# A two-layer attention kernel on one core: additions on GpSimd split into two instructions of two heads each, and TensorE's program put into a loop

## Chip, cores, metric

The kernel runs on one core of a Trainium2 chip. The metric is the device time of one execution in microseconds; the median of three runs is given. All numbers are f32.

## What is computed

For each of 32 images of 128 channels and 32 x 32 = 1024 tokens, the reference computes three stages:

```
x = x + conv_attention(group_norm(x))          # L0: one head of 128 channels, 1024 x 1024 weights
t = tokens(x)
t = t + retrieval_attention(layer_norm(t))     # L1: 8 heads of 16 channels, 1024 x 1024 weights each
t = t + (layer_norm(t) @ w_lora.T) @ W.T       # w_lora is decoded from 4-bit codes
```

In L1, `search_attn = softmax(sq @ sk.T)` for each of the 8 heads, `retrieved = search_attn @ rv` for 2 sets of values, and a small second softmax mixes the two sets. The kernel does not normalise the L1 weights: it takes exponentials of the scores, multiplies them with the values, adds them up over the keys for the denominators, and divides behind that.

## The kernel before

**Phases and steps.** The eight heads of an image are two groups of four (`GROUP = 4`), the 1024 queries are two halves. A group and a half are a phase, so an image has four phases. A phase runs over 8 key tiles of 128 keys; one phase and one key tile are a step, 32 steps an image. In a step TensorE computes four score tiles of 128 keys x 512 queries (`scores`, L791, two entries of two heads each), ACT takes their exponentials out of PSUM into a place of the ring `p1[:, step % 4, n, :]` (L965, four instructions), TensorE multiplies every two steps with the values into `ps_u` (`values`, L805), and GpSimd adds the place to the running sum `p_sum` (`add`, L647), one instruction of 128 x 2048 a step. The first addition of a phase adds the places of steps 0 and 1, so there are 7 a phase and 28 an image. At the end of a phase TensorE multiplies the sum with ones (`den`, L814), ACT copies it out (`den_sb`, L976) and TensorE turns it (`turn_den`, L822).

**The maxima.** Before that TensorE computes the same scores with queries in the rows (`max1`, L771, 64 entries of two matmuls an image), and DVE reduces each bank to a maximum (L1085).

**Order.** Each engine has its order for one turn written out as text (`PE_ORDER`, `ACT_ORDER`, `DVE_ORDER`, `POOL_ORDER`, `SP_ORDER`). An entry such as `scores.8@0/34` is stage, index, how many images ahead of the turn, and for TensorE the PSUM banks. A turn holds 222 entries of TensorE and work of three or four images. `in_order` walks the order: the first turns and the last ones, in which entries of images that don't exist are left out, are written out; the turns between are a loop on the device (`nc.Fori`, 28 turns, with a hint for the back edge) on ACT, DVE, GpSimd and SyncE. TensorE's call has `loop=False`: all its turns are written out. In a written-out turn each wait is against a constant; in a loop it is against a register that is computed from the turn's number.

**Waits.** All engines meet in counting semaphores. On TensorE each entry first waits for its data, then `open_bank` waits until the bank's last reader is done; `max1` and `scores` open two banks, so most of their entries are two bank waits and then two matmuls (TensorE's 663 matmuls and transposes of a turn have 427 waits). `pe.wait_ge` of a bank stands at L660.

**The ring.** GpSimd's addition of a step waits for `p1_ready` (four exponentials more), and for the sum before by `p1_summed`; the first of a phase waits for `den` of the phase before in place of that. ACT writes a place again when the values of the step four before are done (`values_done`) and when its addition is done (`p1_summed`); both are waited for at the first head of a step (n == 0). `den` waits for the seventh addition of its phase.

Of the kernel before, what the change touches and what calls it, by code (L numbers as in the profile page):

```python
# [10 lines left out]
ALU = mybir.AluOpType  # L11
# [9 lines left out]
GROUP = 4  # L21
# [104 lines left out]
def order_of(text):  # L126

    entries = []
    for entry in text.split():
        stage, rest = entry.split(".")  # L130
        index, rest = rest.split("@")
        ahead, _, banks = rest.partition("/")
        entries.append((stage, int(index), int(ahead), tuple(int(bank) for bank in banks)))
    return entries


SECTION = 24
# [61 lines left out]
def wait(engine, sem, value):  # L199

    if not isinstance(value, int) or value > 0:
        engine.wait_ge(sem, value)


def in_order(nc, engine, order, images, stages, banks=None, links=None, section=SECTION, loop=True):


    def turn_of(b):
        for n, (stage, index, ahead, banks_of_entry) in enumerate(order):
            image = b + ahead if isinstance(b, int) else Image(b, ahead, 8 * (n // section + 1))  # L210
            if isinstance(image, Image) or 0 <= image < images:
                if banks:
                    banks.next_image(image)
                    stages[stage](image, index, banks_of_entry)
                else:
                    stages[stage](image, index)

    first = -min(ahead for _, _, ahead, _ in order)
    last = images - 1 - max(ahead for _, _, ahead, _ in order)
    if not loop:  # L220
        for b in range(last + 1 - images, first + images):
            turn_of(b)
        return
    for b in range(last + 1 - images, first):
        turn_of(b)
    before = links.count if links else 0
    turn_of(first)
    per_turn = links.count - before if links else 0
    with nc.Fori(first + 1, last + 1, engines=[engine.engine], hint_back_edge=True) as b:
        if banks:  # L230
            banks.image = Image(b, banks.image - first - 1, 0)
        if links:
            links.looped = (b - first - 1) * per_turn
        turn_of(b)
    if banks:
        banks.image = last + banks.image.ahead
    if links:
        links.looped = (last - first - 1) * per_turn
    for b in range(last + 1, first + images):
        turn_of(b)  # L240


def build(nc, x, norm_w, norm_b, qkv_w, qkv_b, proj_w, proj_b, wq_s, wk_s, wv_r, wq_r, wk_ret, w_out,
          qidx, scales, ffn_w, y):
    images, _, height, width = x.shape
# [6 lines left out]
    ring = 4  # L252
    phases = (HEADS // GROUP) * halves
    steps_per_image = phases * tiles
    adds = tiles - 1
    uses_per_phase = GROUP * tiles_per_half * halves
    maxima = phases * uses_per_phase
    weights_per_image = GROUP * steps_per_image
# [9 lines left out]
    with ExitStack() as ctx:  # L268
        def sb(name, shape, dtype=F32):
            return ctx.enter_context(nc.sbuf_tensor(name, shape, dtype))  # L270
# [4 lines left out]
        def sem(name):  # L275
            return ctx.enter_context(nc.semaphore(name))
# [13 lines left out]
        p1 = sb("p1", [P, ring, GROUP, HALF])  # L290
# [59 lines left out]
        p_sum = sb("p_sum", [P, 2, GROUP, HALF])  # L350
# [148 lines left out]
        def all_images():  # L499
# [39 lines left out]
            max_row1_ready = sem("max_row1_ready")  # L539
            rows_moved = sem("rows_moved")  # L540
            p1_ready = sem("p1_ready")
            p1_summed = sem("p1_summed")
            values_done = sem("values_done")
            u_evicted = sem("u_evicted")
            den_evicted = sem("den_evicted")
# [73 lines left out]
            def gpsimd_program(pool):  # L619
                def norm_rstd(b, index):  # L620
                    pool.wait_ge(var0_ready, 1 * (b + 1))
                    pool.tensor_tensor(scale_shift0[:, 0:1], group0[:, 3:4], minus_half[:, 0:1], ALU.pow)\
                        .then_inc(rstd0_ready, 1)

                def norm_shift(n):
                    def stage(b, index):
                        wait(pool, normed_ready[n], norm_parts * b)
                        pool.wait_ge(var1_ready[n], 1 * (b + 1))
                        pool.tensor_tensor(minus_mean1[:, n, :], minus_sum1[:, n, :], half_col[:, :], ALU.mult)\
                            .then_inc(mean_scaled[n], 1)  # L630
                        pool.tensor_tensor(rstd1[:, n, :], var1[:, n, :], minus_half[:, 0:tiles], ALU.pow)\
                            .then_inc(rstd1_ready[n], 1)
                        pool.wait_ge(mean_scaled[n], 1 * (b + 1))
                        pool.wait_ge(rstd1_ready[n], 1 * (b + 1))
                        pool.tensor_tensor(shift1[:, n, :], minus_mean1[:, n, :], rstd1[:, n, :], ALU.mult)\
                            .then_inc(shift_ready[n], 1)
                    return stage

                def add(b, step):
                    phase, key_tile = divmod(step, tiles)  # L640
                    pool.wait_ge(p1_ready, weights_per_image * b + GROUP * (step + 1))
                    if key_tile == 1:
                        wait(pool, filled["den"], phases * b + phase - 1)
                    else:
                        pool.wait_ge(p1_summed, adds * (phases * b + phase) + key_tile - 1)
                    before = p1[:, (step - 1) % ring, :, :] if key_tile == 1 else p_sum[:, phase % 2, :, :]
                    pool.tensor_tensor(p_sum[:, phase % 2, :, :], before, p1[:, step % ring, :, :], ALU.add)\  # L647
                        .then_inc(p1_summed, 1)

                in_order(nc, pool, order_of(POOL_ORDER), images, {  # L650
                    "norm_rstd": norm_rstd, "ln1_rstd": norm_shift(0), "ln2_rstd": norm_shift(1), "add": add})

            def tensor_program(pe):
                banks = Banks()

                def open_bank(bank, read, each, count, *awaited):

                    before = banks.before(bank)
                    if before and not any(before[0] is other for other in awaited):
                        pe.wait_ge(*before)  # L660
                    banks.take(bank, read, each, count)
                    return ps_bank[:, bank, :]
# [42 lines left out]
                def turn(name, source, ready, each, read):  # L705

                    def stage(b, half, at):
                        done = each if each == 16 else each - 1 + half if name == "mixed_channels" else (half + 1) * each // halves
                        pe.wait_ge(ready, each * b + done)
                        out = open_bank(at[0], read, halves, half + 1)  # L710
                        for i in range(tiles_per_half):
                            last = pe.transpose(out[:, i * P:(i + 1) * P],  # L712
                                                source[:, half * tiles_per_half + i, :], ident[:, :])
                        last.then_inc(filled[name], 1)
                    return stage
# [92 lines left out]
                    last.then_inc(values_done, 1)  # L808

                def den(b, phase, at):  # L810
                    pe.wait_ge(p1_summed, adds * (phases * b + phase + 1))
                    out = open_bank(at[0], den_evicted, phases, phase + 1)
                    for n in range(GROUP):
                        last = pe.matmul(out[n * QUAD:(n + 1) * QUAD, :], ones[:, 0:QUAD], p_sum[:, phase % 2, n, :],  # L814
                                         start=True, stop=True)
                    last.then_inc(filled["den"], 1)
# [8 lines left out]
                def turn_u(b, phase, at):  # L825
# [23 lines left out]
                    "ffn": project_tokens("ffn", ffn_w_sb[:, :], late_channels, late_channels_ready, halves,  # L849
                                          result_ready),  # L850
                    "result": turn("result", t_core, result_ready, halves, out_ready),
                }, banks, loop=False)

            def scalar_program(act):
                read_from = {}
# [3 lines left out]
                def bank_of(stage, index, n=0):  # L859
                    return ps_bank[:, read_from[stage, index][n], :]  # L860
# [95 lines left out]
                def scores(b, index):  # L956
                    step, n = divmod(index, GROUP)
                    if index == 0:
                        act.wait_ge(ffn_w_ready, 1)
                    if n == 0:  # L960
                        wait(act, values_done, visits * b + (step - ring) // 2 + 1)
                        phase, key_tile = divmod(step - ring, tiles)
                        wait(act, p1_summed, adds * (phases * b + phase) + max(key_tile, 1))
                    act.wait_ge(scores_filled[n % 2], weights_per_image // 2 * b + index // 2 + 1)
                    act.activation(p1[:, step % ring, n, :], bank_of("scores", index // 2, n % 2), ACT.Exp, scale=scale1)\  # L965
                       .then_inc(p1_ready, 1)
# [283 lines left out]
```

## Time and profile before

| | |
|---|---|
| median of 3 runs | 4782.99 us (4782.89 to 4784.51) |
| the profiled execution | 4781.04 us, its span 4779.3 us |
| TensorE busy | 4587.4 us, 96%, granted clock 0.984 of full speed |
| GpSimd busy | 4238.1 us, 89% |
| DVE busy | 3881.3 us, 81% |
| ACT busy | 3242.6 us, 68% |

Times in the rows are microseconds from the span's start. PE is TensorE's matmul, PEld its weight load, POOL is GpSimd; a q behind an engine's name (PEldq, POOLq, ACTq) is the engine's sequencer, which executes waits and register operations that stand as instructions of their own (EVENT_SEMAPHORE, ALU_OP, FUSED_REGOPS). A matmul's end is modelled. "issue" is time in which an engine waited for nothing that the profile shows. L numbers are lines of the kernel before.

### The profile page before, as it was taken

Reading aid. Unit: us, or ns where it says so; the run is one execution under the profiler, and the core shown is the slowest. Engines: PE = TensorE matmul, PEld = TensorE weight load, DVE = VectorE, ACT = ScalarE, POOL = GpSimd, SP = SyncE. Lnnn points to the kernel's source line nnn. Section 1 sums busy time; section 2 is a strip of 40 time slices with the busy share of each in tenths; the row PEclk is TensorE's granted clock in tenths of the full one; section 3 lists DMA queues with packets and bytes.
Section 4 is the critical chain, followed back from the end, with each engine's and each line's share of the span. In section 5 each row is a group of like instructions: output and inputs, shape, how many; then the busy total and the mean of one; then the engine's idle time right before and its main releaser. Section 6 shows DMA issues by size and latency. Waiting matters only on the chain.

```text
span 4779.3 us, 95417 instructions
## 1 busy us (share of the span) xinstructions
PE 4587.4 (96%) x29230; PEld 2493.8 (52%) x29230; DVE 3881.3 (81%) x8190; ACT 3242.6 (68%) x6625; POOL 4238.1 (89%) x1142
## 2 busy tenths in 40 slices
PE   5999999999999999999999999999999999999986
PEld 4455555555555555555555555555555555555532
DVE  4788888888888888888888888888888888888773
ACT  2466777766777766777766777766777766777664
POOL 1599999999999999999999999999999999999996
PEclk8899999999999999999999999999999999999987
DMA  1111111111111111111111111111111111111110
GB/s 33 28 41 50 45 32 45 32 45 49 45 32 45 32 45 50 45 32 45 32 45 49 45 32 45 32 45 49 45 32 45 32 45 49 45 32 45 28 41 14
DMA packets 94729, 190.93 MB, mean 40 GB/s; under 512 B 17001, under 2 KB 53481, under 8 KB 94449
## 3 DMA queue, kind: packets, MB, share of 16 engines
q1 hardware_dynamic: 93008, 186.03, 14.0%
q8 instruction: 251, 4.11, 0.4%
q10 hardware_dynamic: 1440, 0.55, 0.0%
q14 instruction: 30, 0.24, 0.0%
HBM read 17.53 MB, written 16.78 MB: 7 GB/s over the span
## 4 chain that ended last, share of the span: by engine, by line
PE 91%; ACT 3%; DVE 2%; POOL 2%; issue 1%; DMA 0%; SPq 0%; ACTq 0%; DVEq 0%; POOLq 0%
PE ps_u L805 19%; PE ps_bank L771 14%; PE ps_bank L791 14%; PE ps_bank L754 10%; PE ps_bank L681 5%; PE ps_bank L692 4%; PE ps_bank L712 3%; PE ps_bank L740 3%; PE ps_bank L814 3%; PE ps_bank L743 3%; PE ps_bank L742 3%; PE ps_bank L741 3%; ACT p L965 2%; POOL p_sum L647 2%; PE ps_bank L723 2%; PE ps_bank L701 2%
## 5 line engine op out<-in xcount | busy, mean ns | idle before, releaser
L647 POOL TENSOR_TENSOR p_sum<-p_sum,p 128x2048 f32<-128x2048 f32 x768 | 3508.4, 4568 | 353.9 <-ACT p L965 306.0
L1085 DVE TENSOR_REDUCE max_part<-ps_bank 128x1 f32<-128x512 f32 x4096 | 2551.3, 681 | 573.5 <-PE ps_bank L771 563.3
L965 ACT ACTIVATE p<-ps_bank 128x512 f32<-128x512 f32 x4096 | 2160.9, 603 | 669.9 <-PE ps_bank L791 653.8
L805 PE MATMUL ps_u<-p,rv 128*32 128x512 f32 x8192 | 996.4, 604 | 0.9 <-ACT p L965 0.9
L771 PE MATMUL ps_bank<-k_stack,q_stack 63*128 63x512 f32 x4096 | 868.9, 452 | 55.2 <-ACT p L965 22.7
L791 PE MATMUL ps_bank<-q_stack,k_stack 64*128 64x512 f32 x4096 | 862.1, 453 | 49.5 <-ACT p L965 29.4
L771 PEld LDWEIGHTS ps_bank<-k_stack,q_stack 63*128 63x128 f32 x4096 | 387.6, 186 | 552.3 <-DVE max_part L1085 244.6
L791 PEld LDWEIGHTS ps_bank<-q_stack,k_stack 64*128 64x128 f32 x4096 | 372.9, 185 | 553.1 <-issue 321.7
L647 POOL TENSOR_TENSOR p_sum<-p 128x2048 f32<-128x2048 f32 x128 | 583.7, 4560 | 66.2 <-ACT p L965 66.2
L754 PE MATMUL ps_bank<-v,p 128*128 128x129 f32 x4096 | 506.8, 277 | 3.1 <-ACT p L920 1.6
L754 PEld LDWEIGHTS ps_bank<-v,p 128*128 128x128 f32 x4096 | 476.0, 191 | 50.1 <-issue 24.0
L805 PEld LDWEIGHTS ps_u<-p,rv 128*32 128x32 f32 x8192 | 215.5, 110 | 463.6 <-issue 450.3
L920 ACT ACTIVATE p<-ps_bank 128x512 f32<-128x512 f32 x512 | 301.5, 594 | 218.3 <-PE ps_bank L743 212.6
L1054 DVE TENSOR_REDUCE max_part<-ps_bank 128x1 f32<-128x512 f32 x512 | 319.2, 679 | 16.4 <-PE ps_bank L723 16.4
L740 PE MATMUL ps_bank<-q_hi,k_hi 128*128 128x512 f32 x512 | 235.0, 459 | 17.1 <-DMA max_row<-max_tile 11.7
L976 ACT COPY den_sb<-ps_bank 128x512 f32<-128x512 f32 x128 | 77.0, 602 | 209.0 <-PE ps_bank L814 209.0
L743 PE MATMUL ps_bank<-q_hi,k_lo 128*128 128x512 f32 x512 | 203.7, 398 | 0.0
L741 PE MATMUL ps_bank<-q_lo,k_hi 128*128 128x512 f32 x512 | 203.6, 398 | 0.0
L742 PE MATMUL ps_bank<-max_row,first_row 128*128 128x512 f32 x512 | 203.3, 397 | 0.0
L723 PE MATMUL ps_bank<-k_hi,q_hi 128*128 128x512 f32 x512 | 163.3, 440 | 1.4 <-ACT k_hi L901 0.8
L814 PE MATMUL ps_bank<-p_sum,ones 128*32 128x512 f32 x1024 | 138.1, 611 | 18.1 <-POOL p_sum L647 17.3
L740 PEld LDWEIGHTS ps_bank<-q_hi,k_hi 128*128 128x128 f32 x512 | 97.3, 190 | 103.7 <-issue 54.8
(143 smaller groups left out, 4231.8 us busy)
## 6 DMA issues: line engine op xcount, KB each, us to landing
k_stack<-k_hi SPq DMA_DIRECT2D x256, 128.0 KB, 2.6
q_stack<-q_hi SPq DMA_DIRECT2D x256, 128.0 KB, 2.8
x_sb<-in_x SPq DMA_DIRECT2D x32, 512.0 KB, 3.6
k_stack<-k_lo SPq DMA_DIRECT2D x128, 128.0 KB, 2.6
q_stack<-q_lo SPq DMA_DIRECT2D x128, 128.0 KB, 2.9
t_held<-t_front SPq DMA_DIRECT2D x32, 512.0 KB, 3.7
rqk<-tok_next SPq DMA_DIRECT2D x32, 512.0 KB, 3.6
t_core<-t_held SPq DMA_DIRECT2D x32, 512.0 KB, 2.9
```

The source lines that it names most:

```text
L647: pool.tensor_tensor(p_sum[:, phase % 2, :, :], before, p1[:, step % ring, :, :], ALU.add)\
L740: pe.matmul(out, k_hi[0][:, keys], q_hi[0][:, queries], start=True, stop=False)
L741: pe.matmul(out, k_hi[0][:, keys], q_lo[0][:, queries], start=False, stop=False)
L742: pe.matmul(out, first_row[:, :], max_row0[:, queries], start=False, stop=False)
L743: pe.matmul(out, k_lo[0][:, keys], q_hi[0][:, queries], start=False, stop=True)\
L754: last = pe.matmul(out[:, 0:P + 1], p0[:, key_tile, i * P:(i + 1) * P], v0[:, key_tile, :], start=(key_tile == 0), stop=(key_tile == tiles ...
L771: pe.matmul(outs[side], q_stack[rows, pair, first:first + P], k_stack[rows, pair, half * HALF:(half + 1) * HALF], start=True, stop=True).t ...
L791: pe.matmul(outs[side], k_stack[rows, pair, keys], q_stack[rows, pair, queries], start=True, stop=True).then_inc(scores_filled[side], 1)
L805: last = pe.matmul(ps_u[n * QUAD:(n + 1) * QUAD, :], rv[:, key_tile, :], p1[:, step % ring, n, :], start=(key_tile == 0), stop=(key_tile = ...
L965: act.activation(p1[:, step % ring, n, :], bank_of("scores", index // 2, n % 2), ACT.Exp, scale=scale1)\
L1054: dve.tensor_reduce(max_part0[:, i, half:half + 1], bank_of("max0", i, half), AXIS.X, ALU.max)\
L1085: dve.tensor_reduce(max_part1[:, phase % 2, i, n, half:half + 1], bank_of("max1", index // 2, side), AXIS.X, ALU.max)\
```

## The change

Three edits. `p1_summed` becomes two semaphores, one for the heads 0 and 1 and one for the heads 2 and 3, and each addition becomes two instructions of 128 x 1024, each with its own wait for its two exponentials and for the half before. ACT waits for the first semaphore at n == 0 and for the second at n == 2; `den` waits for the second alone. TensorE's program goes through the same device loop as the other engines', and the argument `loop` is gone. The orders are the same text.

```
-def in_order(nc, engine, order, images, stages, banks=None, links=None, section=SECTION, loop=True):
+def in_order(nc, engine, order, images, stages, banks=None, links=None, section=SECTION):
...
-    if not loop:
-        for b in range(last + 1 - images, first + images):
-            turn_of(b)
-        return
...
-            p1_summed = sem("p1_summed")
+            p1_summed = [sem(f"p1_summed{part}") for part in range(2)]
...
                 def add(b, step):
                     phase, key_tile = divmod(step, tiles)
-                    pool.wait_ge(p1_ready, weights_per_image * b + GROUP * (step + 1))
                     if key_tile == 1:
                         wait(pool, filled["den"], phases * b + phase - 1)
-                    else:
-                        pool.wait_ge(p1_summed, adds * (phases * b + phase) + key_tile - 1)
-                    before = p1[:, (step - 1) % ring, :, :] if key_tile == 1 else p_sum[:, phase % 2, :, :]
-                    pool.tensor_tensor(p_sum[:, phase % 2, :, :], before, p1[:, step % ring, :, :], ALU.add)\
-                        .then_inc(p1_summed, 1)
+                    for part in range(2):
+                        heads = slice(part * GROUP // 2, (part + 1) * GROUP // 2)
+                        pool.wait_ge(p1_ready, weights_per_image * b + GROUP * step + GROUP // 2 * (part + 1))
+                        if key_tile > 1:
+                            pool.wait_ge(p1_summed[part], adds * (phases * b + phase) + key_tile - 1)
+                        before = p1[:, (step - 1) % ring, heads, :] if key_tile == 1 else p_sum[:, phase % 2, heads, :]
+                        pool.tensor_tensor(p_sum[:, phase % 2, heads, :], before, p1[:, step % ring, heads, :], ALU.add)\
+                            .then_inc(p1_summed[part], 1)
...
                 def den(b, phase, at):
-                    pe.wait_ge(p1_summed, adds * (phases * b + phase + 1))
+                    pe.wait_ge(p1_summed[1], adds * (phases * b + phase + 1))
...
-                }, banks, loop=False)
+                }, banks)
...
                     if n == 0:
                         wait(act, values_done, visits * b + (step - ring) // 2 + 1)
+                    if n % 2 == 0:
                         phase, key_tile = divmod(step - ring, tiles)
-                        wait(act, p1_summed, adds * (phases * b + phase) + max(key_tile, 1))
+                        wait(act, p1_summed[n // 2], adds * (phases * b + phase) + max(key_tile, 1))
```

## Rows read from the trace of the kernel before

**Rows 1.** The page: busy time, the instruction queue, the chain by engine.
```profile
PE 4587.4 (96%) x29230; PEld 2493.8 (52%) x29230; DVE 3881.3 (81%) x8190; ACT 3242.6 (68%) x6625; POOL 4238.1 (89%) x1142
...
q8 instruction: 251, 4.11, 0.4%
...
PE 91%; ACT 3%; DVE 2%; POOL 2%; issue 1%; DMA 0%; SPq 0%; ACTq 0%; DVEq 0%; POOLq 0%
```

**Rows 2.** Windows: busy us by engine (PE, PEld, DVE, ACT, POOL), a turn and the end.
```profile
2402.67:2546.17 143.50, 141.28 (x917) 77.02 (x921) 120.65 (x256) 101.17 (x207) 132.12 (x36) 1.00 0.15 41
...
4620.00:4779.00 159.00, 107.83 (x593) 48.27 (x585) 69.52 (x157) 75.89 (x153) 120.58 (x32) 0.78 0.03 11
```

**Rows 3.** The chain of that turn in order of time: start, us, what.
```profile
2421.00 0.61 ACT p L965
2421.61 0.14 issue
2421.74 0.50 PE ps_bank L771 x2
```

**Rows 4.** That turn's waits of weight loads: us in total, times, longest.
```profile
PEld ps_bank L771 <- DVE max_part L1085: 7.3, 13, 0.8
PEld ps_bank L771 <- ACT p L965: 3.6, 7, 0.8
...
PEld ps_bank L791 <- ACT p L965: 1.7, 4, 0.8
```

**Rows 5.** GpSimd's timeline in that turn: start, us, instructions merged, idle before.
```profile
2400.50 23.17 POOL L647 TENSOR_TENSOR p_sum<-p_sum,p 128x2048 f32<-128x2048 f32 x5 [2.56 <-ACT p L965]
...
2479.36 0.19 POOL L629 TENSOR_TENSOR minus_mean<-minus_sum,half_col 128x8 f32<-128x8 f32 x1
...
2499.99 18.49 POOL L647 TENSOR_TENSOR p_sum<-p_sum,p 128x2048 f32<-128x2048 f32 x4
2518.43 0.56 POOL L622 TENSOR_TENSOR scale_shift<-group,minus_half 128x1 f32<-128x1 f32 x1
```

**Rows 6.** GpSimd's timeline in the last image.
```profile
4685.54 27.97 POOL L647 TENSOR_TENSOR p_sum<-p_sum,p 128x2048 f32<-128x2048 f32 x6 [2.90 <-ACT p L965]
```

**Rows 7.** The chain in the last image.
```profile
4685.54 4.55 POOL p_sum L647
4690.14 0.09 issue
...
4746.05 1.98 PE ps_bank L814 x8
```

**Rows 8.** ACT's timeline in the last image.
```profile
4674.62 4.05 ACT L965 ACTIVATE p<-ps_bank 128x512 f32<-128x512 f32 x8
```

**Rows 9.** The sequencers' instructions by line: count, ns min/median/max, first and last start.
```profile
L660 PEldq EVENT_SEMAPHORE  x179: 51/51/1225, 2403.3 to 2545.5; - x179
...
L645 POOLq ALU_OP  x20: 32/32/32, 2403.8 to 2543.9; - x20
...
L645 POOLq EVENT_SEMAPHORE  x19: 17/17/17, 4640.3 to 4741.4; - x19
...
L202 ACTq ALU_OP  x27: 35/35/35, 2406.2 to 2544.1; - x27
...
L229 ACTq COMPARE_BRANCH  x1: 73/73/73, 588.9 to 588.9; - x1
L229 ACTq BRANCH_PREFETCH_HINT  x1: 31/31/31, 589.2 to 589.2; - x1
```

**Rows 10.** Timelines of ACT and of the weight loads in the same turn.
```profile
2427.53 0.58 ACT L976 COPY den_sb<-ps_bank 128x512 f32<-128x512 f32 x1
...
2428.16 0.42 PEld L822 LDWEIGHTS ps_bank<-ident,den_sb 128*128 128x128 f32 x4 [0.25 <-ACT den_sb L976]
```

**Rows 11.** Around a turn's end: the sequencer's waits (L660), and the weight loads' timeline.
```profile
L660 PEldq EVENT_SEMAPHORE  x2: 51/51/51, 3176.0 to 3178.1; - x2
...
3178.18 0.18 PEld L771 LDWEIGHTS ps_bank<-k_stack,q_stack 63*128 63x128 f32 x2 [0.84 <-DVE max_part L1085]
```

## Prediction

> **What bounds the kernel now.** I read the profile in this order: the page's sums, then one steady turn by windows, then the chain of that turn, then who waits for whom, then GpSimd's timeline, and last the end of the run. The page gives TensorE 96% busy and 91% of the chain, GpSimd 89% busy and 2% of the chain [rows 1]. A steady turn (one image's worth of work) takes 143.50 us, with 141.28 us of TensorE and 132.12 us of GpSimd [rows 2]. TensorE's ends are modelled, so its 141 us hide short waits: the chain of the turn shows where they are. ACT ends an exponential at 2421.61, "issue" takes 0.14 us, then TensorE goes on [rows 3]. I count eleven such "issue" pieces (0.05 to 0.22 us) in the chain of this turn. The list of waits shows more of them, since many lie under the modelled end of the matmul before: 13 + 7 + 4 weight loads of the two score lines wait for a bank that DVE or ACT frees, and some nine more rows of one or two loads each, down from lines such as L822 behind ACT's copy of den_sb, bring it to about 33 [rows 4]. So the steady turn is one stream of TensorE with some 33 handovers in it. GpSimd is not on this chain: it sits idle 2.56 + 3.67 + 0.65 + 0.71 + 2.10 = 9.7 us in the turn, always waiting for exponentials (the first of the five in [rows 5]), and the turn's list of waits has no row in which ACT or TensorE waits for L647. The end is different: in the last image GpSimd is 120.58 us busy of 159 while TensorE falls to 107.83 [rows 2], and from 4685.54 to 4746.05 the chain runs through thirteen additions, one behind the other [rows 6, 7].
>
> **The change part by part, GpSimd.** 28 additions a turn become 56 of 128x1024. The trace has no such shape. From 128x8 (0.19 us, [rows 5]) to 128x2048 (4.57 us) a straight line gives 2.14 ns per column and 0.18 us fixed, so a half takes 2.37 us. Where an instruction does not need the one before it, it starts 0.05 us before that one's end (4 additions from 2499.99 end at 2518.48, the next starts at 2518.43, [rows 5]). Halves alternate, so each depends on the one before the last: two cost 2 x (2.37 - 0.05) = 4.65 us. Today's dependent additions come every (18.49 - 4.57) / 3 = 4.64 us. The sum for the split is nothing, and if all of the overlap is absent it is 0.10 us x 28 = 2.8 us a turn, inside the 9.7 us of idle time. Bounds: without any fixed part 4.57 - 0.10 = 4.47 us (no gain in the turn, as nobody waits); with the 0.56 us of the smallest power row [rows 5] as fixed part of each instruction, 28 x 0.56 = 15.7 us, which is 6 us more than the idle time. The point from which it decides is 9.7 / 28 = 0.35 us an addition.
>
> Starting two heads earlier only shortens waits that cost nothing in the turn. It pays at the end: addition 18 of the last image waits 2.90 us for ACT [rows 6], for the heads 2 and 3 alone, since heads 0 and 1 are the last of the eight exponentials that end at 4678.67 [rows 8]. Its first half fits into that wait (2.37 of 2.90 us), and the thirteen additions behind it, all back to back, move up by 2.3 us. That is the tail's gain; small differences of pitch (4.69 us now, 4.65 with halves) could add 13 x 0.04 = 0.5 us. Take 2.5.
>
> **ACT.** It gets one wait more per step, at n = 2, with a register operation of 35 ns [rows 9]. The sequencer does it while the exponential before (0.61 us, [rows 3]) runs, and the half it asks for was added before. Cost nothing; were each on the path, 32 x 0.035 = 1.1 us a turn.
>
> **TensorE in a loop: the waits.** This is the part that can move the turn. Today every wait of TensorE's is against a constant. An instruction carries one wait; a second one stands in front of it as an instruction of the sequencer, 179 of them in the turn, 51 ns each [rows 9]. Which of the two goes where can be read off GpSimd. In the loop L645 is an ALU_OP that carries the wait for the exponentials, and the addition itself carries the later wait, for the sum before; outside of the loop an EVENT_SEMAPHORE is there, and additions have 0.09 us of "issue" between them [rows 7, 9]: they come every 4.69 us (4685.54, 4690.23), in the loop every 4.64 us [rows 5, 7]. So outside a loop the last wait in program order is the one in the separate instruction, inside a loop the last wait rides on the instruction. For a pair of TensorE (open bank A, open bank B, matmul) the order puts B last, and B is as a rule the one that comes late. Price of a handover through the separate instruction: ACT ends at 2421.61, TensorE starts at 2421.74, 0.13 us [rows 3]. Price of one that rides on the weight load: the copy of den_sb ends at 2428.11, the load starts at 2428.16, 0.05 us [rows 10]. The matmul's start is some 0.03 us behind its load, so the difference is 0.05 to 0.08 us; I take 0.07.
>
> All 33 handovers at 0.07 us would be 2.3 us a turn; only the eleven that the chain shows, 0.8 us. Against this, where the first wait is the late one (about seven, such as L822), it moves off the load onto a register operation and costs some 0.07 us more: 0.5 us. The bounds are thus 0.3 and 1.8 us a turn. A stretch of the path that hops over ACT or DVE skips some handovers, so I stay near the lower one: 0.8 us. The loop runs 28 turns: 22 us.
>
> **TensorE in a loop: registers and branch.** About 400 waits a turn need register values. ACT's and GpSimd's cost 32 to 35 ns each [rows 9], and I allow 40; some 380 x 0.04 = 15 us of the sequencer in place of 179 x 0.051 = 9 us. What hides it: the sequencer stands ahead of the array. At the end of a turn it executes the wait of the next turn's first pair at 3176.0, and that pair's load starts at 3178.18 [rows 11]. The branch itself lasts from 588.9 to about 589.3 on ACT [rows 9], 0.5 us with what follows, under those 2.2 us. Cost nothing; without the cover 28 x 0.5 = 14 us.
>
> A loop could also break the flow of instructions. The instruction queue moved 4.11 MB in 251 packets, 0.4% of 16 engines' span, so 1.2 us a packet [rows 1]; TensorE's program is nearly all of that. One or two packets late at the back edge (1.2 or 2.4 us, and 0.5 us for the branch) against 2.2 us of cover cost nothing or 0.7 us a turn; three in a row cost 1.9 us. The Trainium skill ("Runtime: NRT & Kernel Launch", Instruction fetch mechanics) speaks against the change here: it says that a taken branch to a place outside the fetched window stalls for a fetch, and that TensorE holds 2048 instructions. By the page this turn, longer than that with its register operations, would stall; no row of this trace shows a taken branch of TensorE's, and the shorter loops of the other engines show none.
>
> **Sum.** The profiled execution took 4781.0 us (span 4779.3 and 1.7 around it); the median of the runs is 2.0 above it. 4781.0 - 22 - 2.5 = 4756.5, and with the 2.0 us the forecast of the median is 4758.5 us, 0.5% faster.
>
> **Rivals.**
> 1. Nothing measurable: the late waits are not on the path, or a register wait costs TensorE back what the place of the wait gives. For it: the split itself gives nothing in the turn, and 91% of the chain is named TensorE. Against: the gaps in [rows 3]. Time 4781 (tail alone).
> 2. The back edge stalls: three packets one after the other, 28 x 1.9 = 53 us: 4834 us if the waits give nothing besides, 4812 if they give their 22. Decides from 2.2 us of sequencer time at the edge. For it: no cover beyond that. Against: a prefetch hint stands at the loop's head [rows 9].
> 3. Registers make TensorE slower: every one of the 40 handovers costs 0.02 us more instead of less, 28 x 0.8 = 22 us, 4803 us. For it: the 51 ns of TensorE's separate wait against 17 ns on GpSimd [rows 9], so its sequencer is not the cheapest. Against: the load's own wait needs no extra instruction.
> 4. The halves cost more than the room: 15.7 - 9.7 = 6 us a turn over 31 turns, 186 us more, 4967 us.
> 5. All 33 handovers count, 1.8 us x 28: 4730 us.
>
> **How the numbers follow.** A measurement of this kernel can tell 0.2% (9.6 us) from no change. Chances: the forecast 0.42 (own range 4742 to 4772), rival 5 0.08, rival 1 0.23, rival 2 0.12, rival 3 0.10, rival 4 0.05. Faster: 0.42 + 0.08 = 0.50; same 0.23; slower 0.27. The range leaves out rival 4, the upper half of rival 2 and what is below rival 5: 4728 to 4835.
>
> **What would show it.** Right: a steady turn of about 142.7 us; "issue" pieces of 0.14 us before TensorE shrinking to about 0.05; hardly any EVENT_SEMAPHORE of L660 in the turn and register operations in their place; GpSimd's pair of halves at 4.65 us; the last thirteen additions 2.3 us earlier against the end. Wrong: a gap in TensorE once a turn, at the first pair of the order (rival 2); loads that start later behind ACT's ends than now (rival 3); waits for L647 in the turn (rival 4). The prediction fails if the path of the turn hops over the late waits or if the loop keeps the separate waits.

## The result, and the profile after

The changed kernel takes 4792.52 us (median of 20 runs, 4783.67 to 4801.27), the kernel before 4783.82 us (20 runs, 4781.14 to 4787.95): a ratio of 1.0017 with a 95% interval of 1.001 to 1.0024, 0.17% slower. That is clear of the scatter, but under the 0.2% that the prediction set as the bound of no change; the forecast was 0.5% faster. The profiled execution took 4786.13 us, 5.1 us more than that of before.

The page: busy time, the instruction queue, the chain by engine (against [rows 1]).
```profile
PE 4588.5 (96%) x29230; PEld 2476.0 (52%) x29230; DVE 3882.2 (81%) x8190; ACT 3243.0 (68%) x6625; POOL 4339.4 (91%) x2038
...
q8 instruction: 311, 5.10, 0.4%
...
PE 84%; issue 6%; DVE 5%; ACT 3%; POOL 2%; SPq 0%; DMA 0%; DVEq 0%; ACTq 0%; POOLq 0%
```
TensorE's work is the same, GpSimd has 101 us more of it, and the instruction queue moves 60 packets more than before. Two neighbouring turns by windows, as in [rows 2]:
```profile
2170.50:2314.90 144.40, 141.11 (x915) 76.31 (x914) 120.64 (x256) 101.17 (x207) 135.26 (x64) 1.00 0.15 41
2314.90:2457.70 142.80, 141.07 (x916) 76.31 (x915) 120.71 (x256) 101.17 (x207) 135.33 (x64) 1.00 0.15 42
```
There is no longer one length of a turn. 13 of the 27 turns between two branches take about 142.8 us, 0.7 us less than the turn of before (143.50), and 14 take 144.4 us or more. All busy sums are equal, so the 1.6 us between the two rows is time in which TensorE has nothing to do. The sequencers' instructions of the loop line (count, ns min/median/max, first and last start) say what it is:
```profile
L225 PEldq BRANCH_PREFETCH_HINT  x28: 36/36/45, 448.3 to 4332.6; - x28
...
L225 POOLq COMPARE_BRANCH  x28: 44/49/65, 587.5 to 4470.0; - x28
...
L225 PEldq COMPARE_BRANCH  x28: 87/2542/3918, 591.0 to 4473.6; - x28
```
The same branch takes GpSimd 49 ns and TensorE up to 3.9 us. Its median hides two kinds: 13 branches of 1.27 to 1.77 us and 14 of 3.3 to 3.9 us (the 28th, of 87 ns, is the one that leaves the loop). The two branches that open the windows above, one of each kind:
```profile
L225 PEldq COMPARE_BRANCH  x1: 3358/3358/3358, 2170.6 to 2170.6; - x1
```
```profile
L225 PEldq COMPARE_BRANCH  x1: 1614/1614/1614, 2315.0 to 2315.0; - x1
```
And the weight loads behind each of them (timeline of PEld):
```profile
2171.68 0.16 PEld L812 LDWEIGHTS ps_bank<-p_sum,ones 128*32 128x32 f32 x8
2174.30 0.19 PEld L769 LDWEIGHTS ps_bank<-k_stack,q_stack 63*128 63x128 f32 x2 [2.46 <-issue]
...
2316.11 0.16 PEld L812 LDWEIGHTS ps_bank<-p_sum,ones 128*32 128x32 f32 x8
2317.11 0.19 PEld L769 LDWEIGHTS ps_bank<-k_stack,q_stack 63*128 63x128 f32 x2 [0.84 <-DVE max_part L1084]
```
The array works off `den` until about 2.1 us after the branch began. The short branch (1.61 us) ends inside that cover, and the next pair's load comes 2.1 us after the branch's start, held by DVE and not by the branch. The long one (3.36 us) ends outside: the load comes 3.7 us after its start, with "issue" in front.

Of the 14 long turns 13 take 144.4 to 145.0 us, 144.60 us on average. The other one, which opens with the longest branch of all (3.92 us), takes 146.7 us: in a stretch that begins 5.8 us behind that branch's start TensorE's granted clock is at its lower level (1.2 in place of 2.4 GHz, the value of about 0.5 behind the five busy sums), and up to 1.4 us before that stretch TensorE had stood idle for 2.2 us.
```profile
3320.30:3467.00 146.70, 142.78 (x916) 78.02 (x915) 120.80 (x256) 101.17 (x207) 135.35 (x64) 0.99 0.14 41
3326.10:3329.50 3.40, 3.40 (x18) 3.40 (x17) 2.49 (x7) 1.60 (x4) 2.81 (x2) 0.51 0.00 0
```
Between its fourth image and the loop's end the kernel has this one such stretch, and the kernel before has none there.

The waits came out as forecast. The chain in the turn, at the place of [rows 3], and the sequencer's instructions of the bank wait (L658 now) in 140 us of a turn:
```profile
2419.72 0.60 ACT p L964
2420.37 0.50 PE ps_bank L769 x2
2420.88 0.06 issue
```
```profile
L658 PEldq ALU_OP  x277: 32/32/36, 2420.1 to 2560.0; - x139
L658 PEldq FUSED_REGOPS  x32: 37/46/51, 2422.5 to 2556.1; - x32
L658 PEldq EVENT_SEMAPHORE  x17: 51/51/51, 2428.1 to 2554.2; - x17
```
From the exponential's end to TensorE's start it is now 0.05 us (2420.32 to 2420.37), where it was 0.14 us. Of the separate waits 17 are left in these 140 us; the same stretch of the kernel before has 173, and its whole turn the 179 of [rows 9].

GpSimd's timeline in the last image (the end stands against [rows 6, 7]):
```profile
4688.41 2.37 POOL L645 TENSOR_TENSOR p_sum<-p_sum,p 128x1024 f32<-128x1024 f32 x1
4693.18 25.57 POOL L645 TENSOR_TENSOR p_sum<-p_sum,p 128x1024 f32<-128x1024 f32 x11 [2.40 <-ACT p L964]
4718.72 4.66 POOL L645 TENSOR_TENSOR p_sum<-p 128x1024 f32<-128x1024 f32 x2
4723.35 27.77 POOL L645 TENSOR_TENSOR p_sum<-p_sum,p 128x1024 f32<-128x1024 f32 x12
```
A half takes 2.37 us, a pair of them 4.65 us. The first half of the addition that waited (4688.41) is done inside the wait, and the 25 halves behind it take 57.9 us, to 4751.1, where thirteen additions took 60.5.

One reading trap: the share of "issue" in the chain rose from 1% to 6%, and only a part of this is the branch. Where the chain runs through halves it shows pieces like these, while GpSimd's timeline has no gap there:
```profile
2409.74 2.21 issue
2411.96 2.37 POOL p_sum L645
```
A half waits for the half before the last, so the chain steps back over one that it does not name. A kernel without any loop on TensorE (late_on_load, below) has the same 6%.

### The profile page after: what moved, and what is told of

Same layout as the page of the kernel before. It is cut to its first block, busy times and chain, and to the rows that moved or that the text cites. A ratio compares the mean times of both kernels' runs of the same rounds, so it can differ in the third digit from the quotient of the medians.

```text
span 4784.4 us, 103702 instructions
## 1 busy us (share of the span) xinstructions
PE 4588.5 (96%) x29230; PEld 2476.0 (52%) x29230; DVE 3882.2 (81%) x8190; ACT 3243.0 (68%) x6625; POOL 4339.4 (91%) x2038
## 4 chain that ended last, share of the span: by engine, by line
PE 84%; issue 6%; DVE 5%; ACT 3%; POOL 2%; SPq 0%; DMA 0%; DVEq 0%; ACTq 0%; POOLq 0%
PE ps_u L803 19%; PE ps_bank L769 14%; PE ps_bank L789 13%; PE ps_bank L752 10%; PE ps_bank L679 5%; PE ps_bank L710 3%; PE ps_bank L738 3%; PE ps_bank L812 3%; ACT p L964 2%; PE ps_bank L690 2%; PE ps_bank L741 2%; PE ps_bank L739 2%; PE ps_bank L740 2%; POOL p_sum L645 2%; PE ps_bank L699 2%
## 5 line engine op out<-in xcount | busy, mean ns | idle before, releaser
L645 POOL TENSOR_TENSOR p_sum<-p_sum,p 128x1024 f32<-128x1024 f32 x1536 | 3597.1, 2385 | 256.0 <-ACT p L964 256.0
L769 PEld LDWEIGHTS ps_bank<-k_stack,q_stack 63*128 63x128 f32 x4096 | 377.2, 186 | 574.1 <-ACT p L964 199.5
L645 POOL TENSOR_TENSOR p_sum<-p 128x1024 f32<-128x1024 f32 x256 | 602.1, 2374 | 67.6 <-ACT p L964 67.5
```

The source lines that it names most:

```text
L645: pool.tensor_tensor(p_sum[:, phase % 2, heads, :], before, p1[:, step % ring, heads, :], ALU.add)\
L769: pe.matmul(outs[side], q_stack[rows, pair, first:first + P], k_stack[rows, pair, half * HALF:(half + 1) * HALF], start=True, stop=True).t ...
```

## The experiments

The medians are of five or more runs, each ratio is against the kernel before on the same chip. A turn's length and the branch are read from the profiled execution of each. Of the theories named in the expectations, A puts the loss on the back edge, B on the halves, C on something else that the loop or the orders bring; E says that what decides is where the branch stands in the stream of instructions.

**split_only** and **loop_only** are the two parts of the change alone. split_only gives TensorE's call `loop=False` back:
```
-                }, banks)
+                }, banks, loop=False)
```


> The additions split and the semaphore halved, TensorE's turns written out as before. Theory A (the loop alone makes the difference, with a gain of 0.75 us a turn in its waits and a loss of about 1.0 us a turn at its back edge): a turn of 143.5 us as before, at most 2.5 us gained in the last image, so 4781 to 4784 us. Theory B (the halves on GpSimd cost the 8 us, as its busy time is 101 us more): 4790 to 4794 us, turns of about 143.8 us.


Measured: 4777.57 us (4774.92 to 4781.53), ratio 0.9989 (0.998 to 0.9998). The halves cost nothing, they give 5 us. The last image on GpSimd (timeline, against [rows 6]):
```profile
4677.88 2.36 POOL L649 TENSOR_TENSOR p_sum<-p_sum,p 128x1024 f32<-128x1024 f32 x1
4682.65 25.55 POOL L649 TENSOR_TENSOR p_sum<-p_sum,p 128x1024 f32<-128x1024 f32 x11 [2.42 <-ACT p L968]
```
The span is 5.4 us shorter than before: the wait's end came 2.9 us earlier (4685.54 to 4682.65), and what follows it up to the last addition took 57.9 us in place of 60.5.

loop_only has the loop and undivided additions, with one semaphore. Against the kernel before it is the removal of `loop=False` alone; the cut below is against the changed kernel:
```
-                    for part in range(2):
...
+                    pool.wait_ge(p1_ready, weights_per_image * b + GROUP * (step + 1))
...
+                    pool.tensor_tensor(p_sum[:, phase % 2, :, :], before, p1[:, step % ring, :, :], ALU.add)\
+                        .then_inc(p1_summed, 1)
```


> TensorE in the loop, additions as before. Theory A: turns of 142.8 us where the back edge's branch lasts under 2 us and of 144.4 to 145 us where it lasts over 3 us, 4788 to 4797 us in all. Theory B: 143.5 us a turn or less and 4760 to 4784 us.


Measured: 4814.56 us (4808.33 to 4822.68), ratio 1.0064 (1.005 to 1.0078). In its profile 24 of the 27 branches that are taken are long, where the changed kernel has 14. Behind 9 of the 24 the granted clock is at its lower level for a while, 4.5 to 5.9 us after the branch's start; these nine turns take 146.2 to 146.6 us, the other long ones 144.3 to 144.9. The sum of the parts does not give the whole: the loop alone loses 32 us, beside the halves it loses some 14 (ratio 1.0017 against 0.9989). The branch is the same in both; how often it is long is not, and why the halves should change that is open.

**late_on_load** takes the waits' part without a loop: TensorE's program is written out, and of an instruction's waits the last one in program order is issued first, which puts it on the weight load.
```
+    def issue(self, name, args, kwargs):
+        for sem, value in self.waits[-1:] + self.waits[:-1]:
+            self.inner.wait_ge(sem, value)
+        self.waits = []
+        return getattr(self.inner, name)(*args, **kwargs)
...
+                pe = LateOnLoad(pe)
```


> The additions split, TensorE written out, and of each entry's waits the last in program order is issued first, so that it rides on the weight load and the others stand in front. Theory A: what shortens the turn in the loop is the place of the late wait and nothing else of the loop, so 142.8 us in every turn and no branch: 30 us under the looped kernel, about 4760 us, 0.5% faster than before. Theory C (the looped turn is shorter because register operations replace separate waits of 51 ns, or because of what is fetched): 143.5 us a turn, 4781 to 4784 us.


Measured: 4759.84 us (4758.81 to 4765.38), ratio 0.9955 (0.9941 to 0.9968): within 1.4 us of the forecast, by the forecast's own mechanism, without the loop. Chain and window of a turn (this kernel's matmuls are all recorded on line 218):
```profile
2422.48 0.61 ACT p L991
2423.09 0.04 issue
2423.14 0.99 PE ps_bank L218 x4
...
2412.00:2554.80 142.80, 140.98 (x915) 76.43 (x913) 120.71 (x256) 101.25 (x208) 135.28 (x64) 1.00 0.15 41
```

**two_turns** halves the number of back edges: a pass of TensorE's loop holds two turns.
```
-    with nc.Fori(first + 1, last + 1, engines=[engine.engine], hint_back_edge=True) as b:
+    with nc.Fori(first + 1, last + 1, step=turns, engines=[engine.engine], hint_back_edge=True) as b:
...
-        turn_of(b)
+        for on in range(turns):
+            turn_of(b, on)
```


> The changed kernel with two turns in each pass of TensorE's loop: 14 back edges in place of 28. Theory A: every second turn is 142.8 us for certain, the loss at the edges halves from 29 to about 15 us: 4776 to 4781 us. If the loss is not at the edge but spread over the turn (theory D), 4790 to 4795 us as in the changed kernel.


Measured: 4760.83 us (4760.12 to 4762.33), ratio 0.9955 (0.9941 to 0.9968). That is 15 us or more beyond what the number of edges accounts for, since half of the long branches should have stayed. None did:
```profile
L225 PEldq COMPARE_BRANCH  x14: 88/361/394, 735.8 to 4451.2; - x14
```
So theory A had the right place and the wrong law: the branch costs 0.36 us here. The longer pass also moves the branch, and the kernels below take the two apart.

**Where the branch stands.** The instruction queue moves blocks of 16.4 KB (5.10 MB in 311 packets). The Trainium skill ("Runtime: NRT & Kernel Launch", Instruction fetch mechanics) gives 256 instructions for such a block. The packets have times but no addresses, so which block one holds is read from the order and the number of packets. In two_turns the last packet before the branch, taken to be the loop's first block, is asked for 8.5 to 9.1 us ahead. In the changed kernel it is asked for 0.7 to 1.1 us before the branch where that is short, and 0.9 to 1.6 us after its start where it is long. The instruction queue in the stretch before the branch at 2315.0 (2312.5 to 2315) has one packet:
```profile
q8 instruction: 1, 0.02, 3.1%
```
Before the branch at 2170.6 the last packet lies 11.0 us back, and the next one comes 1.0 us behind the branch's start. One rule fits every slow branch in the traces: it ends 2.3 to 2.9 us after that packet starts, whether it is short or long. This holds for all 27 of the changed kernel, the 27 of loop_only, and the 27 each of slot102 and slot16_no_hint below. A branch is thus as slow as its packet is late. Theory E takes the late request to come from the branch standing just behind the start of a block; no trace shows an instruction's place in its block, so this is tested by moving the branch. Four kernels do so. The argument `head_slot` fills up with empty instructions so that the loop's head has a given place in its block; the trace has 2213 instructions of TensorE's from branch to branch, so a head at 16 puts the branch at place 180, a head at 102 puts it at place 10.
```
-    with nc.Fori(first + 1, last + 1, engines=[engine.engine], hint_back_edge=True) as b:
+    with nc.Fori(first + 1, last + 1, engines=[engine.engine], hint_back_edge=True,
+                 head_slot={engine.engine: 16} if banks else None) as b:
```


> The changed kernel, nothing but the place of TensorE's loop head in the instruction blocks of 256 moved: head at slot 16, so with 2213 instructions a turn the branch stands at slot 180 of its block, about as in the loop of two turns (I estimate slot 180 there and 25 in the changed kernel, from how long before the branch a block was fetched: 8.6 and 1.0 us). Theory E (the branch stalls because its target's block is asked for only when the sequencer enters the branch's own block, 1 us ahead): the branch lasts 0.36 us in all 28 turns, every turn 142.8 us, 4758 to 4764 us. Theory F (28 edges cost what they cost and the loop of two turns was better for another reason): 4785 to 4800 us.


Measured: 4764.95 us (4761.04 to 4767.21), ratio 0.9962 (0.9948 to 0.9976). The branch takes 0.34 to 0.39 us in every turn, but not every turn takes 142.8 us: 25 of 28 take 142.7 to 142.8, one 144.3, and two, in which the granted clock falls to the lower level some 120 us behind the branch, 145.7 and 145.9. The steady part of late_on_load has no such stretch, which is about what separates the two kernels; what makes the clock fall there was not tested.

**slot102** is the same with 102 in place of 16.

> The same with the head at slot 102, the branch at slot 10 of its block, right behind the boundary. Theory E: as in the changed kernel or worse, the branch over 3 us in nearly all turns, 4795 to 4830 us. Theory F: 4785 to 4800 us, as with slot 16.


Measured: 4816.79 us (4812.82 to 4829.03), ratio 1.0079 (1.0065 to 1.0093).

The branch in slot16 and in slot102:
```profile
L225 PEldq COMPARE_BRANCH  x29: 88/361/386, 448.9 to 4452.7; - x29
```
```profile
L225 PEldq COMPARE_BRANCH  x29: 87/3435/3757, 449.9 to 4506.3; - x29
```
The two kernels differ by 86 empty places before the loop and by nothing inside it, and by 52 us. In slot16 the block is asked for 7.9 to 9.2 us ahead, in slot102 always 0.9 to 1.2 us after the branch began. Behind 7 of slot102's 27 long branches the lower clock follows, 4.1 to 5.6 us after the branch's start. (The first of the 29, of 0.33 us, lies ahead of the loop.)

**loop_only_slot16** is loop_only with `head_slot` 16.

> TensorE's loop with the head at slot 16 and additions as before. Theory E: the 32 us that the loop alone lost become a gain of 21: 4760 to 4768 us. If the undivided additions are what makes the loop slow (theory G): still above 4785 us.


Measured: 4768.75 us (4765.33 to 4774.73), ratio 0.9968 (0.9956 to 0.998). The place alone gives loop_only 46 us back, and the halves on top of it give slot16 another 4.

**slot16_no_hint** is slot16 without the instruction that announces the coming back edge.
```
-    with nc.Fori(first + 1, last + 1, engines=[engine.engine], hint_back_edge=True,
+    with nc.Fori(first + 1, last + 1, engines=[engine.engine], hint_back_edge=banks is None,
```


> The kernel after with the head of TensorE's loop at place 16 of its 256-instruction block, as in slot16 (4764.95 us, branch 0.36 us in every turn), and without the hint that names the coming back edge. Theory H, the early request of the target block comes from the hint: without it the branch stalls over 3 us in every turn, the turns go from 142.7 to about 144.5 us or more, and the time is 4800 to 4835 us. Theory I, the sequencer asks for the block behind the branch by itself, so that the hint plays no part: the branch stays at about 0.36 us and the time is 4761 to 4768 us.


Measured: 4825.56 us (4816.28 to 4832.26), ratio 1.0088 (1.0074 to 1.0102). Theory H holds:
```profile
L225 PEldq COMPARE_BRANCH  x29: 83/3454/3844, 448.8 to 4505.1; - x29
...
q8 instruction: 311, 5.10, 0.4%
```
slot16 moved 284 packets: one fewer a turn. Without the hint a packet comes 8.4 to 9.0 us ahead as well, and another 0.9 to 1.1 us after the branch began. The extra packet of each turn fits a first one that holds the block behind the branch, which is not used, and a second one that holds the loop's first block. The branch is about as slow at place 180 without the hint as at place 10 with it; place 10 without it was not run.

**late_no_split** is the kernel before with the waits of late_on_load and undivided additions.

> The kernel before with the late waits on the weight loads, additions undivided, TensorE written out. Theory A: 21 us under before, and 0 to 5 us above the same with divided additions: 4760 to 4766 us. If the gain needs the halves (theory G): near 4783 us.


Measured: 4766.39 us (4763.52 to 4767.54), ratio 0.9963 (0.9949 to 0.9977). The waits alone give 17 us, and the halves add 6 us (late_on_load is 22.7 us below the kernel before on its own chip, this one 16.7).

**late_pairs_only** is late_on_load with the order of the waits turned only in `scores` and `max1`:
```
-        for sem, value in self.waits[-1:] + self.waits[:-1]:
+        for sem, value in self.waits[-1:] + self.waits[:-1] if self.late else self.waits:
```


> TensorE's program written out, halves as in split_only (4777.57 us), but the last wait in program order rides on the weight load only at the entries of scores (and of the maximum) ; the other entries wait as before. Theory J, the gain of late_on_load (4759.84 us, 18 us under split_only) is the sum over the handovers to the scores, which stand behind ScalarE's exponentials: most of it is kept, 4760 to 4767 us. Theory K, the other entries (values, denominators) carry the gain: 4772 to 4778 us.


Measured: 4764.12 us (4761.93 to 4764.5), ratio 0.9955 (0.9941 to 0.9969), as predicted by theory J. Over 26 images of the steady part (from the first exponential of the fourth image on) split_only takes 3728.3 us, late_pairs_only 3716.3, late_on_load 3713.7: the pairs carry 12.0 of the 14.6 us.

## Why the prediction was wrong, step by step

**The failed step is "Cost nothing" for the branch and the back edge.** It had 0.5 us for the branch from ACT's row and one or two packets of 1.2 us, under 2.2 us of cover. The cover was right (2.1 us measured), the branch was not: on TensorE it takes 1.27 to 1.77 us or 3.3 to 3.9 us, and only the first kind fits. The long one is a single packet, not several: 0.9 to 1.6 us pass until it is asked for, and 2.3 to 2.8 us from there to the branch's end. By the turns: 27 of them take 3882.5 us, and would take 27 x 142.77 = 3854.8 us if all were short, so the long branches cost 27.7 us. 13 of the 14 cost 1.83 us each, 23.8 us; the fourteenth, the turn of 146.7 us, is 3.9 us longer, with the lower clock on top. The row the size was taken from was ACT's in a short loop; it cannot hold the case in which the target's block is not there. Rival 2 named this place and priced it at 53 us (1.9 us in each of 28 turns), and half of the turns paid it. That its price of one was nearly right was luck: it was made of three packets of 1.2 us in a row, and the traces show one late packet. The Trainium skill ("Runtime: NRT & Kernel Launch", Instruction fetch mechanics) says that a taken branch outside the fetched window stalls for a fetch. Here the trace agrees for the slow branches, which end 2.3 to 2.9 us after a packet starts. It does not show this as a rule for a long loop: slot16 and two_turns, with the hint, are as long or longer and branch in 0.36 us.

**The waits.** The forecast was 0.8 us a turn, 22 us in all. Turns with a short branch take 142.77 us, 0.73 us less than the turn of [rows 2] and 0.64 us less than the mean turn of before (26 images in 3728.6 us, 143.41 us each): 28 x 0.64 = 18 us, against 22. Two sizes in it were off and partly made up for each other. A handover was priced at 0.07 us, with the matmul 0.03 us behind its load; in the changed kernel's turn load and matmul both start at 2420.37, and the saving is 0.09 us (0.14 to 0.05). By that price 0.64 us is some seven handovers (an estimate), where the forecast had eleven. Without a loop the same order of the waits gives 17 us (late_no_split) and 18 us (late_on_load against split_only). That the late wait then rides on the load, and that this is what the turn gains, is shown.

**The halves in the turn.** A pair was to cost 4.65 us; it comes every 4.66 to 4.68 us there (28.1 us for twelve halves, 27.9 for six undivided additions), so 0.04 us more than an undivided addition or 1 us a turn, which lies in GpSimd's idle time, now 7 us a turn. Rival 4 is refuted by split_only.

**The halves at the end.** Forecast 2.5 us, measured 2.6 us between the wait's end and the last addition (60.5 to 57.9), by the mechanism that was named. The wait's end itself came 2.9 us earlier in split_only, for which the prediction had no term; so the halves are worth 4 to 6 us (three pairs of kernels: 5.0, 6.0 and 3.8). By which path the 2.9 us come was not tried.

**The registers.** Rival 3 is refuted: TensorE's handovers became shorter, not longer, and slot16 with all its register operations is 18 us faster than before.

**ACT's additional wait** cost nothing that shows: ACT's busy time and the turn are as they were.

**The sum, redone.** The profiled execution against before: over the 26 images of the steady part -26 x 0.64 = -17 us for the waits, +12 x 1.83 = +22 us for twelve long branches and +4 us for the one with the lower clock give +9 (measured +9.5); the start up to the fourth image is 3.4 us shorter, the last three images 3.2 us longer, with one more long branch in them, and the time after the last exponential is 4.2 us shorter (43.9 for 48.1 us). Together +5.1 us, the difference of the two executions. The changed kernel's runs spread over 17.6 us, and its median lies 6 us above its profiled run. A number of long branches that varies from run to run would do that, and so would a varying number of stretches at the lower clock. The runs' clocks speak for the second at least in part: the six runs with a mean granted clock of 0.984 or more take 4786.1 to 4791.7 us, the four with 0.981 take 4794.8 to 4801.3. An estimate: 0.003 of 4784 us is about 29 us at half speed, some eight stretches of 3.4 us, and the one in the trace cost 2.1 us (146.7 against 144.60). Only one run has a profile, so neither is shown. What decides between short and long at the place where the changed kernel has its branch is open too. The start's 3.4 us were not looked into.

## What to carry to other kernels

A loop on the device is priced by its branch on that very engine and at that very place: read its duration and the cover behind it, and when a long body's branch is slow, move the loop's head in its block, or hold two turns in a pass, before giving up the loop. A late wait belongs on the instruction itself, not in a separate one in front of it; where the program is written out, the order of two waits decides that, for nothing, and here it was worth 0.37%. And try two parts of a change one by one: the one that was to bring the gain can hide what the other one costs.

## What the hardware showed that was not expected

- The same taken branch of TensorE's took 0.36 us, 1.3 to 1.8 us or 3.3 to 3.9 us, and nothing in the loop had to change for it: 86 places of shift made 52 us of kernel time. On the other engines, whose loops are shorter (63 to 438 recorded instructions a turn), the median was 0.05 to 0.06 us.
- Every slow branch ended 2.3 to 2.9 us after an instruction packet started, with that packet up to 1.1 us before the branch or up to 1.6 us behind its start.
- Behind 1 of the changed kernel's 14 long branches, 9 of loop_only's 24, 7 of slot102's 27 and 2 of slot16_no_hint's 27, TensorE's granted clock fell to the lower level 4 to 6 us after the branch's start, and the turn was about 2 us longer again. What decides which of them was not tested, and slot16 has two such stretches with no long branch near them.
- Of the two places tried, the hint for the back edge helped at one: with the branch at place 180 the target was asked for 8 to 9 us ahead, at place 10 only after the branch began. Without the hint, place 180 is as slow as place 10. Where between the two the change comes, and which place the changed kernel has, no run shows.
- Behind ACT's exponential TensorE starts 0.04 to 0.05 us later where the wait is on its weight load, and 0.14 us later where it is in a separate instruction.
- Two additions of 128x1024, each dependent on the one before the last, come every 4.64 to 4.68 us; one of 128x2048, dependent on the one before, every 4.64 to 4.69 us. Cutting an addition of this size into two cost GpSimd 0.04 us at most.
